# First attention of an early-fusion model: second and third bfloat16 part of q, k and k' on GpSimd, sum of the two attentions on GpSimd, alpha inside the normalizing product

## What is computed

```python
q, k, v, kp = (heads(x @ W.T) for W in (W_Q, W_K, W_V, W_K_prime))   # 16 heads of 16 features
attn   = softmax(q @ k.T / 4)
attn_p = softmax(q @ kp.T / 4)
out = alpha * (attn @ v) + (1 - alpha) * (attn_p @ v)
h = h + out @ W_O.T
```

## Time and profile before

| | |
|---|---|
| median of 3 runs | 2125.05 us (2120.97 to 2126.19) |
| the profiled execution | 2125.76 us, of which the span from first to last instruction is 2124.0 |
| first attention | about 150 to 926 us of the span |
| PE busy | 1830.2 us (86%) |
| VectorE (DVE) busy | 1078.5 us (51%) |
| ScalarE (ACT) busy | 688.6 us (32%) |
| GpSimd (POOL) busy | 328.5 us (15%) |
| largest group on VectorE | ring reductions L854: 768 instructions, 387.9 us, mean 552 ns |
| mean granted TensorE clock | 0.941 of 2.4 GHz |

### The profile page before, as it was taken

One profiled execution on the slowest core, in us unless ns is written; L12 is line 12 of the kernel. 1 busy time (PEld: TensorE's weight loads), 2 busy tenths in 40 slices (PEclk: granted clock), 3 DMA queues, 4 the chain that ended last, 5 costly groups with the idle time before them and its releaser, 6 DMA issues. The chain is left out here.

```text
span 2124.0 us, 30173 instructions
## 1 busy us (share of the span) xinstructions
PE 1830.2 (86%) x10095; PEld 1134.3 (53%) x10095; DVE 1078.5 (51%) x2272; ACT 688.6 (32%) x1288; POOL 328.5 (15%) x289
## 2 busy tenths in 40 slices
PE   5854488888888989958998589999889999999998
PEld 3532133332333333336666356666666676999997
DVE  6544868777777788347776454544332111222221
ACT  0111056454555556734444122323221111011110
POOL 0030000000000000017777121221102221100000
PEclk9876589999999999979999799999999999999999
DMA  4114213212132121010000470000001000344211
GB/s 150 52 50 112 57 35 93 65 47 69 36 89 68 48 68 35 1 46 0 0 0 0 160 247 1 0 0 0 1 1 37 30 27 20 113 141 151 94 35 33
DMA packets 117988, 117.55 MB, mean 55 GB/s; under 512 B 16893, under 2 KB 109823, under 8 KB 117632
## 3 DMA queue, kind: packets, MB, share of 16 engines
q1 hardware_dynamic: 104736, 87.95, 13.9%
q10 hardware_dynamic: 9504, 18.88, 2.5%
q0 software_dynamic: 3648, 9.46, 1.2%
HBM read 80.87 MB, written 35.29 MB: 55 GB/s over the span
## 5 line engine op out<-in xcount | busy, mean ns | idle before, releaser
L854 DVE TENSOR_REDUCE mx<-ps_a 128x1 f32<-128x384 f32 x768 | 387.9, 552 | 88.3 <-PE ps_a L636 81.5
L789 ACT ACTIVATE prob<-ps_a 128x768 f32<-128x768 f32 (+1 forms) x512 | 311.9, 651 | 187.1 <-PE ps_a L650 185.5
L636 PE MATMUL ps_a<-ks,qs 48*128 48x384 bf16 x768 | 138.9, 358 | 104.4 <-DVE mx L854 83.5
L650 PE MATMUL ps_a<-qs,ks 112*128 112x384 bf16 (+1 forms) x768 | 212.9, 338 | 6.0 <-issue 3.9
L1881 PEld LDWEIGHTS ps_e<-xTr,w 128*128 128x128 f32 x1792 | 206.0, 193 | 2.2 <-issue 0.8
L1881 PE MATMUL ps_e<-xTr,w 128*128 128x128 f32 x1792 | 206.3, 276 | 0.6 <-DVE xTr L2054 0.6
L636 PEld LDWEIGHTS ps_a<-ks,qs 48*128 48x128 bf16 x768 | 37.3, 94 | 267.0 <-DVE mx L854 219.0
L1817 PE MATMUL ps_e<-xT_all,w 128*128 (+1 forms) x512 | 169.7, 491 | 0.9 <-ACT xT_all L1908 0.9
L661 PE MATMUL ps_a<-prob,vp 128*32 128x384 f32 x1536 | 167.7, 510 | 0.0
L1103 POOL TENSOR_TENSOR xb_f<-xb_f,xm_f 128x256 f32<-128x256 f32 x24 | 18.1, 752 | 804.6 <-DVE xs_f L1041 804.1
L1817 PEld LDWEIGHTS ps_e<-xT_all,w 128*128 128x128 f32 x512 | 97.5, 192 | 66.5 <-issue 1.8
(11 more groups left out here) (227 smaller groups left out, 2567.1 us busy)
## 6 DMA issues: line engine op xcount, KB each, us to landing
ks<-parts_dram SPq DMA_DIRECT2D x384, 48.0 KB, 2.0
w<-in_L_ffn_W_dram ACTq DMA_DIRECT2D x18, 1024.0 KB, 8.2
parts_dram<-parts SPq DMA_DIRECT2D x24, 576.0 KB, 3.3
qs<-parts_dram SPq DMA_DIRECT2D x192, 48.0 KB, 2.0
pix<-in_x_dram SPq DMA_DIRECT2D x24, 256.0 KB, 4.8
w<-in_L_ffn_W_dram SPq DMA_DIRECT2D x6, 1024.0 KB, 12.1
grouped_x<-empty_row SPq DMA_DIRECT2D x1, 4352.0 KB, 23.9
grouped_h<-empty_row SPq DMA_DIRECT2D x1, 4240.5 KB, 35.8
```

Source lines behind the costliest of these rows:

```text
L636: pe.matmul(ps[:, (r + side) % 3, 0:T], qs[rows, b, hh, t * P:(t + 1) * P], ks[rows, b, kp, hh], start=True, stop=True, tile_position=(sid ...
L650: mm = pe.matmul(ps[:, 4 + t, 0:T], ks[rows, b, kp, hh, t * P:(t + 1) * P], qs[rows, b, hh], start=True, stop=True)
L789: act.activation(prob[:, g % 2, j, ts.start:ts.stop], ps[:, 4 + ts.start:4 + ts.stop, 0:T], ACT.Exp).then_inc(exp_done.sem, 1)
L854: dve.tensor_reduce(mx[:, half, kp, side * QUAD + q, t:t + 1], ps[:, (r + side) % 3, 0:T], AX.X, ALU.max).then_inc(ring_free.sem, 1)
```

## The change

The rounding of `rest` and the second difference move from VectorE to GpSimd, which has its own `low_parts` for every projection, in the order of the steps. VectorE counts `rest_done` when the remainder is made; PE's bank 3 waits for `rest_done`, not `parts_done`. SyncE's stores still wait for `parts_done`, now counted by GpSimd, and VectorE still waits for the part two before. The addition of the two kinds moves to GpSimd (`add_kinds`, `ys_done`); `turn_y` waits for `ys_done`, and VectorE's product of an odd group waits for the sum before it. In `normalize` the multiplication of the reciprocal with alpha is dropped and alpha becomes the scalar of one `scalar_tensor_tensor`, (outputs * alpha) * reciprocal.

```diff
+            @block.gpsimd
+            def _(pool):
+                def low_parts(i, n):
+
+                    m, a = n // KC, n % KC
+                    pool.wait_ge(rest_done.sem, rest_done.at(i, n + 1))
+                    if a == 0 and (not isinstance(i, int) or i):
+                        pool.wait_ge(scr_out[m].sem, scr_out[m].at(i, 0))
+                    pool.sem_inc(part_free.sem, 1)
+                    pool.tensor_copy(parts[:, m, 1, a], rest[:, a]).then_inc(part_step.sem, 1)
+                    pool.wait_ge(part_step.sem, part_step.at(i, n + 1))
+                    pool.tensor_tensor(parts[:, m, 2, a], rest[:, a], parts[:, m, 1, a], ALU.subtract
+                                       ).then_inc(parts_done.sem, 1)
+
+                def add_kinds(i, q):
+
+                    pool.wait_ge(y_done.sem, y_done.at(i, 2 * q + 2))
+                    to = y[:, :, q * QUAD * D0:(q + 1) * QUAD * D0].rearrange("p t (j d) -> p t j d", j=QUAD)
+                    pool.tensor_tensor(to, to, y2[:], ALU.add).then_inc(ys_done.sem, 1)
+
+                def turn(i, b, prev, more, more2):
+                    for v in range(UNITS):
+                        step, n, of = bank3(v, prev, more, more2)
+                        if step == "turn_outputs" and n % 2:
+                            add_kinds(i + of, n // 2)
+                        elif step == "project":
+                            low_parts(i + of, n)
+
+                for n in range(3 * KC):
+                    low_parts(0, n)
+                for n in range(3 * KC):
+                    low_parts(1, n)
+                for_images(pool, turn)
+                add_kinds(B - 1, GROUPS // 2 - 1)
...
                 def turn_y(i, k):
-                    pe.wait_ge(y_done.sem, y_done.at(i, GROUPS))
+                    pe.wait_ge(ys_done.sem, ys_done.at(i, GROUPS // 2))
...
-                         "project": (project, parts_done), "output": (output, h_done)}
+                         "project": (project, rest_done), "output": (output, h_done)}
...
                     dve.scalar_tensor_tensor(rest[:, a], ps[:, bank, 0:T], scale, parts[:, m, 0, a],
-                                             ALU.mult, ALU.subtract).then_inc(part_step.sem, 1)
-                    dve.wait_ge(part_step.sem, part_step.at(i, 2 * n + 1))
-                    dve.tensor_copy(parts[:, m, 1, a], rest[:, a]).then_inc(part_step.sem, 1)
-                    dve.wait_ge(part_step.sem, part_step.at(i, 2 * n + 2))
-                    dve.tensor_tensor(parts[:, m, 2, a], rest[:, a], parts[:, m, 1, a], ALU.subtract
-                                      ).then_inc(parts_done.sem, 1)
+                                             ALU.mult, ALU.subtract).then_inc(rest_done.sem, 1)
...
                     dve.reciprocal(rec[:], o[:, :, :, D0]).then_inc(y_step.sem, 1)
-                    dve.wait_ge(y_step.sem, y_step.at(i, n + 1))
-                    dve.tensor_scalar(rec[:], rec[:], al[:, kp:kp + 1], None, ALU.mult).then_inc(y_step.sem, 1)
-                    dve.wait_ge(y_step.sem, y_step.at(i, n + 2))
-                    over = rec[:].unsqueeze(3).to_broadcast([P, TT, QUAD, D0])
-                    if kp == 0:
-                        dve.tensor_tensor(to, o[:, :, :, 0:D0], over, ALU.mult).then_inc(y_done.sem, 1)
-                    else:
-                        dve.tensor_tensor(y2[:], o[:, :, :, 0:D0], over, ALU.mult).then_inc(y_step.sem, 1)
-                        dve.wait_ge(y_step.sem, y_step.at(i, n + 3))
-                        dve.tensor_tensor(to, to, y2[:], ALU.add).then_inc(y_done.sem, 1)
+                    dve.wait_ge(y_step.sem, y_step.at(i, g + 1))
+                    if kp == 1:
+                        dve.wait_ge(ys_done.sem, ys_done.at(i, q))
+                    dve.scalar_tensor_tensor(y2[:] if kp else to, o[:, :, :, 0:D0], al[:, kp:kp + 1],
+                                             rec[:].unsqueeze(3).to_broadcast([P, TT, QUAD, D0]), ALU.mult, ALU.mult
+                                             ).then_inc(y_done.sem, 1)
```

More of the change, by code:

```diff
@@ L495, in attention0 @@
         xn_done, xt_done, xT_done = sig("xn_done", TT), sig("xt_done", KC), sig("xT_done", KC)
-        proj, hi_done, part_step = sig("proj", 3 * KC), sig("hi_done", 3 * KC), sig("part_step", 6 * KC)
+        proj, hi_done, part_step = sig("proj", 3 * KC), sig("hi_done", 3 * KC), sig("part_step", 3 * KC)
+        rest_done, ys_done = sig("rest_done", 3 * KC), sig("ys_done", GROUPS // 2)
+        part_free = sig("part_free")
         parts_done, pv_done, v_done = sig("parts_done", 3 * KC), sig("pv_done", 2), sig("v_done", 2)
@@ L505, in attention0 @@
         av_done, o_done, oT_done = sig("av_done", GROUPS), sig("o_done", GROUPS), sig("oT_done", GROUPS)
-        y_step, y_done = sig("y_step", 5 * GROUPS // 2), sig("y_done", GROUPS)
+        y_step, y_done = sig("y_step", GROUPS), sig("y_done", GROUPS)
         yt_done, yT_done, op_done, h_done = sig("yt_done", KC), sig("yT_done", KC), sig("op_done", 2), sig("h_done0", 2)
@@ L702, in turn @@
                 def turn(i, b, prev, more, more2):
-                    last = (y_done, i - 1, GROUPS - 2) if prev else (parts_done, 1, 3 * KC)
+                    last = (y_done, i - 1, GROUPS - 2) if prev else (rest_done, 1, 3 * KC)
                     for v in range(UNITS):
@@ L870, in normalize @@
                     q, kp = g // 2, g % 2
-                    n = 5 * q + 2 * kp
                     o = ps[:, 3, 0:T].rearrange("p (t j e) -> p t j e", t=TT, j=QUAD)
```

## The result

The median of four runs is 2063.7 us (2060.01 to 2065.15), against 2125.62 us (2120.97 to 2129.39) of the kernel before beside it. The ratio is 0.9707, with a 95% interval of 0.9684 to 0.973: faster by 62 us. The direction and the place were right, the size was too small. The profiled execution took 2060.01 us with a span of 2058.2, so its span is 65.8 us shorter than that of before (2124.0).

What follows compares the result with a forecast made beforehand. Bound by PE's hand-written order waiting for VectorE in the first attention. Turns' low parts -31.4, first ring -5.6, normalize -6.3, start +2.0, end 0: -41.3 us, from 2125.8 to 2084.5 us; own range 2078 to 2091, whole range 2073 to 2104.

Steps and rivals of the forecast that it cites:

- The turns: First attention, turns 0 to 5: 5.23 us a turn from the low parts, about 1.0 from normalization; 36.9 us gained.
- The first ring: Image 0's ring, interleaved with image 1's projections: six waits for the reduction each 0.93 us shorter, 5.6 us gained.
- rival E: More than counted: fewer stalls raise the first ring's granted clock, or further short waits go; some 10 us more, 2074; 6 in 100.
- What bounds the kernel: First attention: PE's hand-written order, idling nearly always for VectorE; ten idle times make 8.3 us of an 85.60 us turn.
- The six waits: PE behind a turn's six projections: 1.94, 0.99, 1.44, 1.37, 0.52, 0.98 us fall to about 1.0, 0.1, 0.5, 0.4, 0, 0.1.
- Normalize: VectorE saves 0.27 us on an even and 0.66 on an odd group; PE gains 1.0 us a turn, 6.3 in sum.
- GpSimd's pair: Cast 0.65 plus subtraction 1.0, 1.75 us with handover (ends 1.3 and 3.5); covered in the turns, 2.0 us lost at the start.
- The end: Last addition at the first attention's end: about 0.55 us on GpSimd plus handover, against 0.27 saved; 0 within 0.1.
- Rival A: GpSimd's instructions shut VectorE out, so reductions behind remainders wait for the whole pair; 20 us slower, 2146 us; 5 in 100.
- B: GpSimd's cast and subtraction take 3.5 us; the start loses 11 us instead of 2; 2094 us; 10 in 100.
- C: In the turns, ScalarE's exponentials or the ring's own rhythm end last, so half the gain remains; 2105 us; 12 in 100.
- D: The parts' way through DRAM (store, stacks, maxima in SP's queue) sets the turn's length; nothing changes, 2125; 3 in 100.

Runs made afterwards that it cites:

- the transposes: Kernel before with 1 to 8 unused TensorE transposes ahead of the scores at six places behind projections in the turns: 2119.76 us against 2125.12, ratio 0.9963.
- VectorE's time given back: Kernel after with an unused reduction of 0.91 us added on VectorE behind each remainder: 2101.77 us, ratio 0.988.
- `warm`: Unused TensorE transposes of the identity added in the first ring: kernel before 2121.97 us, ratio 0.9962; kernel after 2063.88 us, ratio 0.9698.
- the loop written out: Kernel after with the first attention's device loop over images 1 to 4 written out: 2056.62 us, ratio 0.9669.
- normalize alone: Kernel after with the low parts whole on VectorE, as in the kernel before: 2116.09 us, ratio 0.9949.

## Why the prediction was right in direction and wrong in size

**The step that failed** is the sum's own rule: it counted only PE's idle time, and took the durations of PE's instructions as fixed, read from turn 4, whose clock was 1.00. The runs showed that the waits cost more than their length: behind them PE's instructions ran at a lower granted clock, and the change gave that back too, some 8 us in the turns and 5 in the first ring. That is most of both terms that were mis-sized.

*The turns* (-36.9 forecast, -49.3 measured). At full clock the turn fell by 6.92 us (86.01 to 79.09), where 6.23 had been counted. That is 0.69 in each of six, 4.1 us; by its parts, the low parts were counted a little high (5.23, measured 4.89), normalize low (1.0, measured 1.40), and together they gave 0.6 more than the two alone. Turn 0 had been counted 0.5 lower than the others, but fell by no less (7.99). The rest, 12.4 - 4.1 - 0.5 = 7.8 us, goes with the clock. Turn by turn it is much like what the kernel before gets back when half of the waits is filled: beyond the 6.92 us, turns 1, 2, 4 and 5 lost 2.77, 2.76, 0 and 1.45 us by the change, and 2.81, 2.79, 0.03 and 1.42 by the transposes. The agreement to a tenth is luck, since a turn in one trace is a microsecond or more shorter where a fall happens to be missing, and turn 3 doesn't take part in it (6.67 us shorter by the change, 2.39 longer with the transposes). That several microseconds go with the clock is not luck: the kernel with VectorE's time given back lost its clock again.

*The first ring* (-5.6 forecast, -11.0 measured). The 0.93 to a projection was measured at 1.0, six times some 6.0. The other 5.0 us are, nearly all, projections at 2.4 GHz that had run at 1.2. That the clock follows from fewer waits is shown in the turns by experiments. In the ring it is shown less well: `warm` sped up some of the projections and not the whole. It rests there on the two groups of ring lengths, 78 to 79 against 67 to 70, and on the ring of 74.8 us when VectorE's time was given back.

The prediction had this as rival E, with the right mechanism, but only in the first ring, and not in the turns, where the larger half of it lay; it priced E at 10 us and gave it 6 in 100. It was worth 13 us. The rows for a better chance were to be had: the turns before turn 4 lie in the same trace with clocks of 0.96, 2.8 us longer for the same instructions. Looking at one turn hid it.

**Point by point, the rest.**

- *What bounds the kernel:* right. The waits went where rows 3 were. Of turn 4's 11.9 us of idle time 5.3 are left: 1.8 in the rest of three of those waits, and 3.6 that had not been counted on.
- *The six waits:* forecast 1.0, 0.1, 0.5, 0.4, 0 and 0.1 us; measured 0.95, 0, 0.45, 0.38, 0 and 0. The two waits for bank 3 would have been worth 0.58 us a turn by themselves, not 1.51.
- *Normalize:* the joined instruction was taken at 0.36 us with up to 0.1 more as the bound, and it measured 0.418 (first row below). PE gained more all the same, 1.40 us a turn. The addition on GpSimd carries 0.36 of it.
- *GpSimd's pair:* the cast 0.505 us (forecast 0.65, within its bounds of 0.45 and 1.0), the subtraction 0.914 (forecast 1.0). So the bfloat16 outputs came no dearer than the float32 rows had led to expect. Against VectorE's 0.36 and 0.56 us these are factors of 1.4 and 1.6, where the prediction's estimate of 1.8 us for the pair had used 1.96. At the start the remainders came 1.29 us apart and GpSimd took a part every 1.44 us, back to back, where 1.75 had been forecast. VectorE had made one every 1.46 us, so the start lost 0.2 us, not 2.0.
- *The end:* 0 had been forecast, and it is 0.5 us shorter. PE waits 1.53 us for the last addition where rows 10 have 1.47.
- *Rival A (GpSimd shuts VectorE out):* out. The ring's reductions have a mean of 551 ns (552 before), the remainders 557. *B:* the pair is 1.4 us; the price of B was well judged, since with a pair of 3.2 us the start was 10.1 us longer than before's, against 11 forecast for 3.5. *C (half comes back):* no wait for the exponentials took the place of those for VectorE. *D (the way through DRAM):* PE's only wait for a transfer is that of the start, 19.3 us.

The kernel after, DVE and POOL instructions by line and form (busy, mean ns, idle before):

```profile
L886 DVE TENSOR_REDUCE mx<-ps_a 128x1 f32<-128x384 f32 x768 | 388.1, 551 | 95.1 <-PE ps_a L673 88.8 <-DVE mneg L895 0.3
...
L914 DVE SCALAR_TENSOR_TENSOR y<-ps_a,al,rec 128x192 f32<-128x192 f32 x64 | 26.7, 418 | 3.8
...
L875 DVE SCALAR_TENSOR_TENSOR rest<-ps_a,parts 128x384 f32<-128x384 f32 x48 | 26.8, 557 | 70.2 <-ACT parts L798 70.2
```

```profile
L602 POOL TENSOR_TENSOR parts<-rest,parts 128x384 bf16<-128x384 f32 x48 | 43.9, 914 | 3.9
...
L600 POOL CAST parts<-rest 128x384 bf16<-128x384 f32 x48 | 24.2, 505 | 284.6 <-DVE rest L875 284.6
...
L609 POOL TENSOR_TENSOR y<-y 128x192 f32<-128x192 f32 x32 | 19.0, 594 | 337.7 <-DVE y L914 337.7
```

## What to carry to other kernels

Where PE works most and its waits are short and many, read the granted clock of every repeat of a stage, not of one: a repeat at 0.96 beside one at 1.00 with the same instructions says that the waits cost more than their length, here a fifth on top in the turns (7.8 us over 41.5) and some eight tenths in the first ring (5.0 over 6.0; about 2 over 6 in the trace with the loop written out, where the clock rose later). Price a moved instruction by who stands behind it: the 0.93 us that left the chain ahead of a reduction was gained nearly whole, while freeing the bank sooner by itself moved most of the wait to the next reduction. Work that goes to an idle engine is free in the steady part of the loop as far as its cover reaches (3.2 us to a part was covered here, and no longer one was tried), and is paid where the pipeline fills.

## What was not expected of the hardware

**A busy PE at the low clock.** In the kernel before with `warm` in the first ring, the part behind the projections, by stretch:

```profile
222.00:250.00 28.00, 26.53 (x98) 9.68 (x99) 24.47 (x50) 0.00 (x0) 0.00 (x0) 0.52 0.31 86
```

The same part of the kernel after, without:

```profile
222.00:250.00 28.00, 11.79 (x48) 2.39 (x46) 24.85 (x50) 0.00 (x0) 0.00 (x0) 0.50 0.14 36
```

PE was busy for 26.53 of 28 us and was granted 0.52, while in the turns 74 of 79 us went with 1.00. VectorE sets the pace of this part (24.5 us busy in both), which is why nothing was lost. Why the clock stayed low here is left open, and with it the second reason for which the ring's experiment missed. The transposes alone don't explain it: in the same trace, PE did nothing else from 168 to 176 us and was granted 1.00.

**The turn of a loop costs more than its stall.** PE stood 3.94 us for it, once, and the turn of the kernel was 5.8 us longer than with the loop written out.

**GpSimd slowed one kind of VectorE instruction, off the path.** The tensor_scalar of the layernorm reads one input from SBUF. Beside the first pairs, at the start of the stage, it took up to 1070 ns, where before had at most 415:

```profile
L864 DVE TENSOR_SCALAR xn<-h,mv,rstd x24: 405/410/1070, 146.6 to 650.9; 128x256 f32<-128x256 f32 x12, 128x256 f32 x12
```

In the kernel with normalize alone, which has no pairs there, the longest is 414 ns. The Trainium skill ("SBUF — State Buffer", Who interferes with whom) names, beside instructions with two SBUF inputs, those in a two-port mode, which a tensor_scalar can enter. No row shows whether this one was in it; the trace fits so far, since this one is slowed and the reductions and remainders, with an input from PSUM, are not. It happened only where image 1's rows were normalized ahead of need, and the start lost 0.2 us in all.
